# Two fused layers on one core: new constants for the hand-planned order of steps, which place the scatter and gather DMAs of GpSimd otherwise among its other steps

## The chip, the cores and the metric

One Trainium2 chip, of which the kernel uses one core. The metric is the device time of one execution in microseconds; the kernel before was run three times beside this work, and the median of those runs is the time before.

## What is computed

The input is `x`, 16 sequences of 512 tokens with 128 channels. Two layers follow each other, each with a mixer and a mixture of experts on the same normalised input, multiplied together and added to the residual:

```
xn = layernorm(x);  s = rwkv6_mixer(xn);        g = silu(experts0(xn));  x = x + s * g
xn = layernorm(x);  s = attention16heads(xn);   g = silu(experts1(xn));  x = x + s * g
# experts: scores = xn @ router; top 2 of 8; each expert is (silu-gated up, gate) then down, width 256
# experts0: softmax over the two; experts1: sigmoid gate on the input of the expert, and one shared expert
# rwkv6: token-shift mixes (five low-rank "lora" terms), decay = exp(-exp(w)), a 64x64 state per head, group norm, gate
```

## The kernel before

Each sequence is one batch `n` (0 to 15). Per batch and layer the work is cut into steps: tuples `(n, layer, kind, ...)`. A table `DUE` gives each step a due time, worked out by `due_times()` from the constants at the head of the file. One batch is due `PERIOD` = 167.91 after the last, and layer 1 of a batch runs beside layer 0 of the batches behind it. Each engine has a queue of its own, an in-order program: `order(engine)` sorts all steps by `due(step) + LATER[engine][kind]`, and an engine issues for each step what that step has for it, or nothing. So the constants are no waits and no times on the chip: they only set the order of the steps in the five queues (PE, ACT, DVE, POOL, SP). What starts when is up to semaphores.

The kinds that matter here:

- Layer 0's mixer is a chain, `mixin`, `lora`, `decay`, `proj`, `value`, `diag`, `pair`, `level` 0 to 4, `cross128/256/512`, `wkvsum`, `wkv`, `wkvT`, `finish`. A `level` i multiplies 32 small 64x64 products on PE (L740). Between its two halves of 16 stands a fence: PE waits until the last product of the first half has raised a semaphore. Its operand `rk` (two buffers, `mixa` and `rk_odd`) is made in step `decays` i: POOL writes differences (L1140, L1141), ACT takes their exponential (L1028), POOL multiplies it in (L1155, twice).
- Experts. `route` and `rank` find for each token its two places in a list sorted by expert. `scatter` 0 to 7 are eight indirect DMAs that POOL issues (L1112), which write 128 token rows each to those places in HBM (for layer 1 two products `xgate`, L1108, come ahead of the first and the fifth). `fetch` 0 to 3 read the sorted rows back (SP, L558), `weights` read the weights of the block's expert (SP, three DMAs each, L573 to L575), `xT` transposes on PE (L653), `up`, `gate`, `down` are the expert's products, `yout` writes the result to HBM (SP, L584), and `gather` 0 to 7 are eight indirect DMAs of POOL (L1123) that bring each token its two rows. `combine` adds them.
- Layer 1's attention: `smax` (PE L828, row maxima on DVE L1360), `soft` (PE L843, exponential on ACT L1007), `pv` (PE L857), then `headsT` (PE L864), `outT` (PE L613) and `finish` (PE L806), with ACT copies between (L1015, L1017). `mrow` sends the row maxima through two SP DMAs.

The lines that place the steps which the change moves:

```
due[0, "decays", s[2]] = due[s] - DECAYS_BEFORE              # levels; CROSS_BEFORE for cross*
due[layer, "gather", i] = due[layer, "yout", QUADS - 1] + GATHER_AFTER + GATHER_EVERY * i
due[layer, "scatter", i] = due[layer, "rank"] + SCATTER_AFTER + SCATTER_EVERY * i
due[layer, "fetch", m] = max(due[layer, "scatter", 2 * NT - 1] + FETCH_AFTER, due[layer, "xT", m] - FETCH_BEFORE)
due[1, "headsT", g] = soft_at + PV_AFTER + HEADS_AFTER       # outT, finish: LAST_AFTER later each
at -= UNITS0_EARLY                                           # in due(): experts of batch 0, layer 0
return sorted(PLAN, key=lambda s: due(s) + LATER[engine].get(s[2], 0.0))
```

Of the kernel before, what the change touches and what calls it, by code (L numbers as in the profile page):

```python
# [66 lines left out]
PERIOD = 167.91  # L67
MIX_START = 0.91
MIX_EVERY = 5.92
DECAYS_BEFORE = 5.86  # L70
CROSS_BEFORE = 5.77
FINISH_AFTER = 4.27
UNIT_START = 4.02
UNIT_EVERY = 9.78
GATE_AFTER = 2.82
DOWN_AFTER = 8.1
XT_BEFORE = 4.7
WEIGHTS_BEFORE = 17.22
GATHER_AFTER = 8.11
COMBINE_AFTER = 29.52  # L80
YOUT_AFTER = -0.18
NORM0_AT = 100.17
NORMT_AFTER = 4.16
ROUTE_AFTER = 1.7
RANK_AFTER = 4.58
SCATTER_AFTER = 1.7
FETCH_AFTER = 7.18
LAYER1_AFTER = 20.48
NORM1_AFTER = 2.85
ROUTE1_AFTER = 8.52  # L90
# [32 lines left out]
def due_times():  # L123
# [1389 lines left out]
```

## Time and profile before

| | us |
|---|---|
| median of 3 runs | 2964.4 |
| lowest and highest of them | 2952.69, 2973.52 |
| the profiled execution, its own time | 2970.36 |
| span of its core in the profile | 2968.6 |
| PE busy | 2538.9 (86%) |
| DVE, ACT, POOL busy | 1713.8, 1411.3, 996.5 |
| mean granted TensorE clock, share of full | 0.946 |

The profiled execution lies 6.0 us above the median, and 1.8 us of its time lie outside the span. In the views below, times are in us from the start of the span, PE is the matmul engine, PEld its weight load, and square brackets give how long an engine stood idle ahead of an instruction and what the profile names as its releaser.

### The profile page before, as it was taken

The numbers are of one execution on the slowest core, as the hardware profiler recorded it, in microseconds if no ns is written. First come the engines' busy times: TensorE is split into PE (matmuls) and PEld (weight loads), VectorE is DVE, ScalarE is ACT, GpSimd is POOL, SyncE is SP. The second block draws the span as 40 slices with busy tenths as digits, with TensorE's granted clock in tenths as the row PEclk, the third lists the DMA queues.
The fourth block names the chain that finished last, engine by engine and source line by source line (L and its number), as shares of the span: only waits on it lengthen the run. The fifth ranks groups of instructions, "written<-read, shape, count | busy, mean of one in ns | idle before, by whom it ended". The sixth has DMA issues, their size and how long they took to land.

```text
span 2968.6 us, 54716 instructions
## 1 busy us (share of the span) xinstructions
PE 2538.9 (86%) x18122; PEld 1773.5 (60%) x18122; DVE 1713.8 (58%) x4229; ACT 1411.3 (48%) x2613; POOL 996.5 (34%) x1140
## 2 busy tenths in 40 slices
PE   5688898888989888898888989888898888988987
PEld 3456565665656666566665656666566565656644
DVE  3355566565566656656565566656556565565653
ACT  1235454455445454454444445455454454445554
POOL 2433342423433233342323433243342323433201
PEclk6789999999999999999999999999999999999998
DMA  4234333333343333433333333333433333333222
GB/s 132 66 107 116 115 98 109 104 109 110 103 115 98 104 110 104 121 102 99 109 99 110 103 108 92 116 107 108 117 99 102 102 107 109 105 108 89 86 61 67
DMA packets 384820, 306.24 MB, mean 103 GB/s; under 512 B 37440, under 2 KB 376096, under 8 KB 384544
## 3 DMA queue, kind: packets, MB, share of 16 engines
q1 hardware_dynamic: 368160, 269.16, 31.1%
q0 software_dynamic: 16384, 33.59, 4.1%
q8 instruction: 151, 2.47, 0.4%
q14 instruction: 125, 1.02, 0.1%
HBM read 247.15 MB, written 54.39 MB: 102 GB/s over the span
## 4 chain that ended last, share of the span: by engine, by line
PE 64%; issue 12%; ACT 8%; DVE 7%; another core or an unknown queue 5%; POOL 2%; DMA 0%; SPq 0%; ACTq 0%; POOLq 0%; DVEq 0%
PE bank_st L843 7%; PE bank_s L828 7%; PE bank_y L688 6%; PE bank_pv L857 6%; PE bank_h L669 6%; PE bank_mix L740 5%; PE bank_g L669 5%; ACT probs L1007 3%; PE bank_mix L699 2%; DVE rowmax L1360 2%; ACT ks L992 2%; PE bank_mix L709 1%; PE bank_attn L864 1%; PE bank_mix L653 1%
## 5 line engine op out<-in xcount | busy, mean ns | idle before, releaser
L1360 DVE TENSOR_REDUCE rowmax<-bank_s 128x1 f32<-128x512 f32 x1016 | 699.1, 688 | 511.2 <-PE bank_s L828 405.2
L1007 ACT ACTIVATE probs<-bank_st 128x512 f32<-128x512 f32 x992 | 589.7, 594 | 356.6 <-PE bank_st L843 324.0
L843 PE MATMUL bank_st<-qs,ks 128*128 128x512 f32 x992 | 508.7, 513 | 67.2 <-ACT probs L1007 53.5
L828 PE MATMUL bank_s<-ks,qs 128*128 128x512 f32 x1016 | 451.7, 445 | 99.1 <-DVE rowmax L1360 78.4
L828 PEld LDWEIGHTS bank_s<-ks,qs 128*128 128x128 f32 x1016 | 198.9, 196 | 196.0 <-DVE rowmax L1360 141.2
L843 PEld LDWEIGHTS bank_st<-qs,ks 128*128 128x128 f32 x992 | 194.5, 196 | 196.9 <-ACT probs L1007 126.3
L1123 POOL DMA_INDIRECT yg<-ys_d,index x256 | 248.9, 972 | 181.1 <-DMA ys_d<-y_sb 111.5
L688 PEld LDWEIGHTS bank_y<-wbuf,hid 128*128 128x128 f32 x1920 | 260.9, 201 | 61.5 <-DVE hid L1254 27.1
L669 PEld LDWEIGHTS bank_h<-xT_sb,wbuf 128*128 128x128 f32 x1920 | 256.6, 197 | 57.9 <-issue 25.4
L669 PE MATMUL bank_h<-xT_sb,wbuf 128*128 128x128 f32 x1920 | 269.9, 284 | 18.0 <-DVE th L1242 17.2
L688 PE MATMUL bank_y<-wbuf,hid 128*128 128x128 f32 x1920 | 275.3, 288 | 10.7 <-ACT y_sb L932 6.8
L669 PEld LDWEIGHTS bank_g<-xT_sb,wbuf 128*128 128x128 f32 x1920 | 257.7, 196 | 44.6 <-issue 26.7
L924 ACT ACTIVATE th<-bank_h 128x512 f32<-128x512 f32 (+1 forms) x288 | 164.7, 572 | 220.7 <-PE bank_h L669 190.1
L1242 DVE SCALAR_TENSOR_TENSOR th<-th,bank_h 128x512 f32<-128x512 f32 (+1 forms) x288 | 187.8, 652 | 141.4 <-ACT th L924 134.4
L669 PE MATMUL bank_g<-xT_sb,wbuf 128*128 128x128 f32 x1920 | 266.3, 282 | 0.0
L1254 DVE TENSOR_TENSOR hid<-th,bank_g 128x512 f32<-128x512 f32 (+1 forms) x288 | 187.7, 652 | 119.2 <-remote 68.6
L857 PE MATMUL bank_pv<-probs,v 128*32 128x512 f32 x2048 | 252.6, 612 | 1.2 <-ACT probs L1007 1.0
L1070 POOL TENSOR_TENSOR xmixT<-moved,xnT 128x512 f32<-128x512 f32 x80 | 86.8, 1086 | 395.8 <-DVE moved L1284 395.8
L992 ACT ACTIVATE ks<-bank_attn,cols_sb 32x512 fp32r<-32x512 f32 x256 | 173.4, 677 | 36.7 <-PE bank_attn L820 34.2
L1112 POOL DMA_INDIRECT xs_d<-xn,index x128 | 126.2, 986 | 108.5 <-PE bank_mix L758 42.3
L1112 POOL DMA_INDIRECT xs_d<-xgate,index x128 | 127.2, 994 | 35.1 <-issue 26.1
L1155 POOL TENSOR_TENSOR mixa<-kT,expd 128x256 f32<-128x256 f32 x48 | 36.6, 762 | 293.6 <-ACT expd L1028 293.6
(243 smaller groups left out, 3634.5 us busy)
## 6 DMA issues: line engine op xcount, KB each, us to landing
wbuf<-up SPq DMA_DIRECT2D x480, 128.0 KB
wbuf<-gate SPq DMA_DIRECT2D x480, 128.0 KB
wbuf<-down SPq DMA_DIRECT2D x480, 128.0 KB
xs_sb<-xs_d SPq DMA_DIRECT2D x96, 256.0 KB
ys_d<-y_sb SPq DMA_DIRECT2D x96, 256.0 KB
xs_sb<-xs_d SPq DMA_DIRECT2D x32, 192.0 KB
ys_d<-y_sb SPq DMA_DIRECT2D x32, 192.0 KB
x_next<-x SPq DMA_DIRECT2D x16, 256.0 KB, 3.2
```

The costliest lines, as they stand in the source:

```text
L669: last = mm(ps[:, (FT * i + f) * P:(FT * i + f + 1) * P], wbuf[:, load % WRING, part, f * P:(f + 1) * P], rows, start=True, stop=True)
L688: last = mm(bank[YB][:, blk % 4 * P:(blk % 4 + 1) * P], hid[:, NUMBER[n, layer, "up", u] % 4, (FT * i + f) * P:(FT * i + f + 1) * P], wbuf ...
L828: mm(room(s, b)[:], qs[:, slot, q * P:(q + 1) * P], ks[:, slot, j, :], start=True, stop=True).then_inc(filled[b], 1)
L843: mm(room(s, b)[:], ks[:, slot, j, k * P:(k + 1) * P], qs[:, slot, :], start=True, stop=True).then_inc(filled[b], 1)
L857: last = mm(ps[32 * j:32 * j + 32, :], v1_all[:, k, (DK + 1) * (HG * g + j):(DK + 1) * (HG * g + j) + VCOLS], probs[:, slot, j, :], start= ...
L992: last = A(ks[rows, group % RING, j, :], ps[rows, :], ACT.Identity, bias=cols_sb[rows, COL_KONE:COL_KONE + 1])
L1007: A(probs[:, turn % PRING, h % HG, :], ps[:], ACT.Exp).then_inc(emptied[b], 1)
L1112: pool.indirect_dma_start(xs_d[layer][:, :], where, src, None).then_inc(scattered[layer], 16)
L1123: pool.indirect_dma_start(yg[layer][:, k, q, :], None, ys_d[layer][:, :], where).then_inc(gathered[layer], 16)
L1242: v.scalar_tensor_tensor(out=th[:, i % 2, 0:wide], in0=th[:, i % 2, 0:wide], scalar=1.0, in1=bank[HB][:, 0:wide], op0=ALU.add, op1=ALU.mul ...
L1254: v.tensor_tensor(hid[:, i % 4, 0:wide], th[:, i % 2, 0:wide], ps[:, 0:wide], ALU.mult).then_inc(emptied[GB], 1)
L1360: v.reduce_max(rowmax[:, h // HG % 2, NT * (h % HG) + q:NT * (h % HG) + q + 1], content(s, b)[:], AX).then_inc(emptied[b], 1)
```

## The change

Only constants move; no instruction is added or taken away, and no wait.

```
-DECAYS_BEFORE = 5.86            +DECAYS_BEFORE = 4.34
-CROSS_BEFORE = 5.77             +CROSS_BEFORE = 6.35
-FINISH_AFTER = 4.27             +FINISH_AFTER = 7.19
-GATHER_AFTER = 8.11             +GATHER_AFTER = 8.53
-SCATTER_AFTER = 1.7             +SCATTER_AFTER = 1.11
-SCATTER_EVERY = 3.18            +SCATTER_EVERY = 3.16
-FETCH_AFTER = 7.18              +FETCH_AFTER = 6.83
-FETCH_BEFORE = 19.53            +FETCH_BEFORE = 21.15
-HEADS_AFTER = 1.74              +HEADS_AFTER = 2.1
-UNITS0_EARLY = -2.61            +UNITS0_EARLY = -4.82
 LATER['pool']: scatter 0.48 -> 0.21, finish, headsT, xT, value, diag (POOL has nothing in these five)
 LATER['pe']:   wkvT 0.75 -> 1.45
 LATER['act']:  diag, down;  LATER['dve']: attnv, fetch;  LATER['sp']: decay, norm, cross256, cross512
                (these engines have nothing to issue in those steps)
```

`FINISH_AFTER` is not used by `due_times()`.

Put through `due_times()` and `order()`, the new constants give the following in a batch in the middle of the run (s = scatter, g = gather, | = other POOL steps; layer 1's scatters are of batch n, its gathers of batch n-1):

```
POOL, layer 1  before  s0 | s1 s2 | s3 | s4 g0 s5 g1 g2 s6 g3 | g4 s7 g5 g6 g7 |
               after   s0 s1 | s2 | s3 | s4 s5 g0 g1 s6 g2 | g3 s7 g4 g5 g6 g7 |
POOL, layer 0  before  decays2 | g0 | decays3 | g1 g2 g3 g4 | decays4 | g5 g6 g7 |
               after   decays2 | g0 g1 | decays3 | g2 g3 g4 | decays4 | g5 g6 g7 |
POOL, layer 0's scatters: s0 | decays7 | s1 s2 s3 s4 s5 s6 s7, before and after
```

On ACT `decays` 0, 1, 3 and 4 come one to three steps later and `decays` 5 one earlier; on PE four pairs of neighbours change places (`headsT` 3 and `level` 1, `outT` and `level` 2, layer 1's `finish` and a `soft`, `wkvT` and a `smax`); on SP `fetch` goes ahead of the `yout` that it stood behind, in five places; DVE's order stays. In batch 0 ten mixer steps of PE come ahead of an expert step that they stood behind.

## Rows read from the trace of the kernel before

**Rows 1.** The page: busy time by engine, and the chain that ended last by engine.

```profile
PE 2538.9 (86%) x18122; PEld 1773.5 (60%) x18122; DVE 1713.8 (58%) x4229; ACT 1411.3 (48%) x2613; POOL 996.5 (34%) x1140
PE 64%; issue 12%; ACT 8%; DVE 7%; another core or an unknown queue 5%; POOL 2%; DMA 0%; SPq 0%; ACTq 0%; POOLq 0%; DVEq 0%
```

**Rows 2.** Windows: first batch, a middle one; busy by engine, granted clock, DMA.

```profile
31.00:147.00 116.00, 78.58 (x581) 54.75 (x581) 47.46 (x127) 25.87 (x49) 45.08 (x54) 0.72 0.29 86
...
1011.00:1190.00 179.00, 155.58 (x1132) 110.24 (x1132) 106.60 (x263) 88.03 (x164) 62.34 (x72) 0.96 0.37 106
```

**Rows 3.** Groups of PE instructions: busy, mean ns, idle before and its releasers.

```profile
L740 PE MATMUL bank_mix<-mixa 64*64 64x64 f32 x1536 | 65.4, 224 | 8.4 <-PE bank_mix L740 4.6 <-ACT xT_sb L917 0.7 <-POOL mixa L1155 0.3
...
L740 PE MATMUL bank_mix<-rk_odd 64*64 64x64 f32 x1024 | 43.6, 224 | 22.0 <-remote 11.2 <-PE bank_mix L740 6.7 <-issue 3.0
```

**Rows 4.** Waits: who waited for whom, us in total, times, longest.

```profile
PE bank_s L828 <- issue: 16.8, 14, 2.8
...
PE bank_st L843 <- issue: 10.4, 11, 3.2
```

**Rows 5.** Timeline of POOL, `gather` 1 to 4 of layer 0, batch 6.

```profile
1116.33 0.99 POOL L1123 DMA_INDIRECT yg<-ys_d,index  x1
...
1120.12 1.02 POOL L1123 DMA_INDIRECT yg<-ys_d,index  x1 [0.30 <-issue]
```

**Rows 6.** Timeline of PE in the same stretch: `headsT` 3, then `level` 3.

```profile
1109.80 0.63 PE L864 MATMUL bank_attn<-ident_sb,oT 128*128 128x128 f32 x4 [0.37 <-ACT v L957]
...
1119.20 0.68 PE L740 MATMUL bank_mix<-rk_odd 64*64 64x64 f32 x16
1122.14 0.68 PE L740 MATMUL bank_mix<-rk_odd 64*64 64x64 f32 x16 [2.25 <-remote]
```

**Rows 7.** Timeline of all engines around layer 0's scatters (batch 7's).

```profile
1147.49 1.02 POOL L1112 DMA_INDIRECT xs_d<-xn,index  x1 [0.17 <-issue]
...
1155.13 0.96 POOL L1112 DMA_INDIRECT xs_d<-xn,index  x1 [0.30 <-issue]
1157.68 0.60 ACT L1015 ACTIVATE oT<-bank_pv 128x512 f32<-128x512 f32 x1 [5.31 <-remote]
...
1158.33 1.12 PE L864 MATMUL bank_attn<-ident_sb,oT 128*128 128x128 f32 x4 [2.95 <-ACT oT L1015]
```

**Rows 8.** Timeline of all engines around layer 1's first long run of DMAs.

```profile
1044.94 1.00 POOL L1112 DMA_INDIRECT xs_d<-xgate,index  x1 [0.28 <-DMA ys_d<-y_sb]
...
1052.67 0.96 POOL L1123 DMA_INDIRECT yg<-ys_d,index  x1 [0.30 <-issue]
...
1054.69 0.50 PE L843 MATMUL bank_st<-qs,ks 128*128 128x512 f32 x1 [3.25 <-issue]
```

**Rows 9.** Timeline of all engines, `decays` 0 and `level` 0, later `decays` 3.

```profile
1097.06 0.62 ACT L1028 ACTIVATE expd<-moved 128x512 f32<-128x512 f32 x1
...
1097.76 0.84 POOL L1155 TENSOR_TENSOR mixa<-kT,expd 128x256 f32<-128x256 f32 x1 [13.82 <-ACT expd L1028]
...
1098.56 0.84 POOL L1155 TENSOR_TENSOR mixa<-rT,expd 128x256 f32<-128x256 f32 x1
...
1100.03 0.59 ACT L1007 ACTIVATE probs<-bank_st 128x512 f32<-128x512 f32 x1
...
1101.78 1.43 PE L740 MATMUL bank_mix<-mixa 64*64 64x64 f32 x32
...
1116.45 0.60 ACT L1007 ACTIVATE probs<-bank_st 128x512 f32<-128x512 f32 x1 [1.76 <-PE bank_st L843]
```

**Rows 10.** Timeline of all engines around `wkvT` (L613).

```profile
1177.58 0.69 DVE L1360 TENSOR_REDUCE rowmax<-bank_s 128x1 f32<-128x512 f32 x1 [0.59 <-PE bank_s L828]
...
1178.07 0.60 PE L613 MATMUL bank_mix<-ident_sb,kT 128*128 128x128 f32 x4
```

**Rows 11.** Timeline of all engines, `fetch` 2 of layer 0 and its `xT`.

```profile
1057.59 0.44 SPq L558 DMA_DIRECT2D xs_sb<-xs_d  x1
...
1069.06 0.63 PE L653 MATMUL bank_mix<-ident_sb,xs_sb 128*128 128x128 f32 x4 [0.81 <-DVE moved L1284]
```

More of the change, by code:

```diff
@@ L69 @@
 MIX_EVERY = 5.92
-DECAYS_BEFORE = 5.86
-CROSS_BEFORE = 5.77
-FINISH_AFTER = 4.27
+DECAYS_BEFORE = 4.34
+CROSS_BEFORE = 6.35
+FINISH_AFTER = 7.19
 UNIT_START = 4.02
@@ L78 @@
 WEIGHTS_BEFORE = 17.22
-GATHER_AFTER = 8.11
+GATHER_AFTER = 8.53
 COMBINE_AFTER = 29.52
@@ L85 @@
 RANK_AFTER = 4.58
-SCATTER_AFTER = 1.7
-FETCH_AFTER = 7.18
+SCATTER_AFTER = 1.11
+FETCH_AFTER = 6.83
 LAYER1_AFTER = 20.48
@@ L95 @@
 MROW_AFTER = 3.09
-HEADS_AFTER = 1.74
+HEADS_AFTER = 2.1
 LAST_AFTER = 5.4
-SCATTER_EVERY = 3.18
+SCATTER_EVERY = 3.16
 GATHER_EVERY = 1.5
@@ L101 @@
 MIX0_STEP = 0.0
-UNITS0_EARLY = -2.61
+UNITS0_EARLY = -4.82
 SOFT0_EARLY = 0.0
@@ L106 @@
 ROUTE15_EARLY = 4.71
-FETCH_BEFORE = 19.53
-LATER = {'dve': {'up': 1.19, 'gate': 1.0, 'level': 0.61, 'decay': 1.3, 'lora': 0.51, 'rank': 0.96, 'yout': -0.03, 'pv': 1.08, 'headsT': 0.92, 'attnv': 0.21, 'diag': -0.69, 'cross128': -0.85, 'stack': 1.61, 'cross512': -1.5, 'wkvT': 0.22, 'mixed': 0.83, 'wkvsum': 0.17, 'shared': -0.25, 'route': 0.68, 'fetch': 0.12, 'combine': 0.94, 'scatter': -0.91, 'finish': -2.01, 'normT': -0.31, 'weights': -0.97, 'pair': -0.66, 'qk': 0.05, 'xT': 0.18, 'value': -1.11, 'gather': 0.83, 'wkv': 1.02, 'decays': -0.46, 'outT': 0.52, 'down': 0.66, 'proj': -0.01}, 'act': {'soft': -0.4, 'decays': -0.16, 'gate': 0.72, 'finish': -1.63, 'outT': 2.61, 'mrow': 0.8, 'rank': -0.51, 'smax': 0.1, 'shared': -0.63, 'weights': -1.41, 'fetch': 0.93, 'value': 0.47, 'combine': -0.19, 'up': -0.06, 'level': -0.5, 'mixin': 0.06, 'wkvT': 2.81, 'headsT': 0.62, 'cross128': 1.15, 'norm': 2.72, 'mixed': 0.54, 'yout': -0.32, 'gather': 0.75, 'stack': -0.03, 'attnv': 0.27, 'diag': -0.41, 'pv': -1.12, 'lora': 0.98, 'scatter': 0.89, 'down': 0.2, 'normT': 0.17, 'pair': 0.61, 'cross512': 0.01}, 'pool': {'lora': -1.03, 'wkvT': -0.34, 'down0': 1.07, 'headsT': -2.95, 'wkv': 0.87, 'down': -0.67, 'norm': 0.26, 'fetch': -0.44, 'pv': 0.56, 'stack': 1.51, 'gate': -1.54, 'outT': 0.22, 'normT': 0.23, 'soft': 0.86, 'qk': 1.09, 'yout': 0.5, 'cross256': 1.22, 'gather': 0.28, 'level': 5.46, 'value': -0.54, 'up': 1.08, 'smax': 0.59, 'mrow': 0.0, 'cross128': -1.44, 'weights': 0.48, 'combine': 0.14, 'shared': -1.46, 'decay': -0.87, 'diag': 0.67, 'route': 0.92, 'proj': 1.78, 'scatter': 0.48, 'decays': -0.54, 'rank': -1.12, 'xT': -0.02, 'mixed': 1.5, 'attnv': -0.39, 'wkvsum': -1.17, 'pair': -0.8, 'cross512': -0.72, 'finish': -0.57, 'mixin': 1.01}, 'pe': {'down': -0.56, 'soft': -0.2, 'level': 0.0, 'gate': 1.03, 'mixed': -0.07, 'normT': 0.48, 'proj': -0.12, 'wkvT': 0.75, 'up': 0.21, 'attnv': -0.33, 'norm': -0.47, 'diag': -2.09, 'value': -0.57, 'cross256': 1.31, 'pair': -0.57, 'mixin': 1.17, 'wkv': -0.5, 'finish': -0.86, 'mrow': -0.23, 'shared': -1.42, 'fetch': 1.19, 'route': 0.22, 'weights': 2.33, 'yout': 1.2, 'gather': -1.28, 'xT': 0.01, 'rank': 0.39, 'cross128': -0.53, 'wkvsum': 0.78, 'qk': -0.11, 'lora': 0.06, 'scatter': 0.33, 'cross512': 1.26, 'decays': 0.12, 'combine': 0.27, 'decay': 0.06, 'stack': -0.29, 'outT': 0.54}, 'sp': {'soft': 0.1, 'norm': 2.82, 'wkvsum': 2.2, 'finish': 0.27, 'decays': -1.59, 'mrow': -0.49, 'rank': 0.41, 'pair': 2.37, 'stack': 0.26, 'smax': -0.96, 'level': 0.63, 'weights': -1.04, 'gather': 1.03, 'normT': -1.83, 'wkvT': -0.6, 'lora': -0.96, 'pv': -0.41, 'fetch': 2.87, 'up': 0.34, 'attnv': -2.24, 'value': 1.67, 'proj': 3.2, 'yout': 0.01, 'qk': 1.58, 'cross128': 0.14, 'route': 0.54, 'mixin': 2.03, 'xT': 0.98, 'down': -1.0, 'diag': 0.12, 'combine': 0.01, 'decay': 2.0, 'gate': -1.06, 'shared': 0.02, 'mixed': 0.3, 'headsT': -1.99, 'scatter': -0.38, 'cross256': -0.41}}
@@ new lines @@
+FETCH_BEFORE = 21.15
+LATER = {'dve': {'up': 1.19, 'gate': 1.0, 'level': 0.61, 'decay': 1.3, 'lora': 0.51, 'rank': 0.96, 'yout': -0.03, 'pv': 1.08, 'headsT': 0.92, 'attnv': -0.54, 'diag': -0.69, 'cross128': -0.85, 'stack': 1.61, 'cross512': -1.5, 'wkvT': 0.22, 'mixed': 0.83, 'wkvsum': 0.17, 'shared': -0.25, 'route': 0.68, 'fetch': 0.21, 'combine': 0.94, 'scatter': -0.91, 'finish': -2.01, 'normT': -0.31, 'weights': -0.97, 'pair': -0.66, 'qk': 0.05, 'xT': 0.18, 'value': -1.11, 'gather': 0.83, 'wkv': 1.02, 'decays': -0.46, 'outT': 0.52, 'down': 0.66, 'proj': -0.01}, 'act': {'soft': -0.4, 'decays': -0.16, 'gate': 0.72, 'finish': -1.63, 'outT': 2.61, 'mrow': 0.8, 'rank': -0.51, 'smax': 0.1, 'shared': -0.63, 'weights': -1.41, 'fetch': 0.93, 'value': 0.47, 'combine': -0.19, 'up': -0.06, 'level': -0.5, 'mixin': 0.06, 'wkvT': 2.81, 'headsT': 0.62, 'cross128': 1.15, 'norm': 2.72, 'mixed': 0.54, 'yout': -0.32, 'gather': 0.75, 'stack': -0.03, 'attnv': 0.27, 'diag': -0.68, 'pv': -1.12, 'lora': 0.98, 'scatter': 0.89, 'down': -0.92, 'normT': 0.17, 'pair': 0.61, 'cross512': 0.01}, 'pool': {'lora': -1.03, 'wkvT': -0.34, 'down0': 1.07, 'headsT': -3.85, 'wkv': 0.87, 'down': -0.67, 'norm': 0.26, 'fetch': -0.44, 'pv': 0.56, 'stack': 1.51, 'gate': -1.54, 'outT': 0.22, 'normT': 0.23, 'soft': 0.86, 'qk': 1.09, 'yout': 0.5, 'cross256': 1.22, 'gather': 0.28, 'level': 5.46, 'value': 0.04, 'up': 1.08, 'smax': 0.59, 'mrow': 0.0, 'cross128': -1.44, 'weights': 0.48, 'combine': 0.14, 'shared': -1.46, 'decay': -0.87, 'diag': 1.65, 'route': 0.92, 'proj': 1.78, 'scatter': 0.21, 'decays': -0.54, 'rank': -1.12, 'xT': 1.11, 'mixed': 1.5, 'attnv': -0.39, 'wkvsum': -1.17, 'pair': -0.8, 'cross512': -0.72, 'finish': -1.08, 'mixin': 1.01}, 'pe': {'down': -0.56, 'soft': -0.2, 'level': 0.0, 'gate': 1.03, 'mixed': -0.07, 'normT': 0.48, 'proj': -0.12, 'wkvT': 1.45, 'up': 0.21, 'attnv': -0.33, 'norm': -0.47, 'diag': -2.09, 'value': -0.57, 'cross256': 1.31, 'pair': -0.57, 'mixin': 1.17, 'wkv': -0.5, 'finish': -0.86, 'mrow': -0.23, 'shared': -1.42, 'fetch': 1.19, 'route': 0.22, 'weights': 2.33, 'yout': 1.2, 'gather': -1.28, 'xT': 0.01, 'rank': 0.39, 'cross128': -0.53, 'wkvsum': 0.78, 'qk': -0.11, 'lora': 0.06, 'scatter': 0.33, 'cross512': 1.26, 'decays': 0.12, 'combine': 0.27, 'decay': 0.06, 'stack': -0.29, 'outT': 0.54}, 'sp': {'soft': 0.1, 'norm': 4.73, 'wkvsum': 2.2, 'finish': 0.27, 'decays': -1.59, 'mrow': -0.49, 'rank': 0.41, 'pair': 2.37, 'stack': 0.26, 'smax': -0.96, 'level': 0.63, 'weights': -1.04, 'gather': 1.03, 'normT': -1.83, 'wkvT': -0.6, 'lora': -0.96, 'pv': -0.41, 'fetch': 2.87, 'up': 0.34, 'attnv': -2.24, 'value': 1.67, 'proj': 3.2, 'yout': 0.01, 'qk': 1.58, 'cross128': 0.14, 'route': 0.54, 'mixin': 2.03, 'xT': 0.98, 'down': -1.0, 'diag': 0.12, 'combine': 0.01, 'decay': 2.25, 'gate': -1.06, 'shared': 0.02, 'mixed': 0.3, 'headsT': -1.99, 'scatter': -0.38, 'cross256': -2.32, 'cross512': -0.87}}
```

## The prediction

> **What bounds the kernel now.** I read the page first. PE is busy 86% of the span and has 64% of the chain, with 12% "issue" and 5% "another core or an unknown queue" [rows 1]. So PE sets the time, and what can be won is its idle time. The windows say how much that is: in a middle batch PE is busy 155.58 of 179 us, at a granted clock of 0.96, so some 23 us of a batch are idle, while in the first batch, where only one mixer chain is under way, it is busy 78.58 of 116 [rows 2]. Since every queue is in order, a moved step costs or gives something only where PE then stands idle longer or shorter.
>
> The second question was where those 23 us lie. The groups of PE show that the five `level` steps, all of one form and one length, are not treated alike: those that read `rk_odd` (levels 1 and 3) lose 22.0 us over the run, of which the largest part is put down to "remote" and to the step's own fence, those that read `mixa` (0, 2 and 4) only 8.4 [rows 3]. The timeline shows the place: in batch 6 the first half of `level` 3 starts at 1119.20 and the second half at 1122.14, after 2.25 us in which PE waits for its own product behind the fence, released by nobody the profile knows [rows 6]. At that moment POOL is in the fourth of four `gather` DMAs that follow each other, from 1116.33 to 1121.14 [rows 5]. The same shows larger beside the seven `scatter` DMAs of layer 0 in a row, 1147.49 to 1156.09: ACT stands 5.31 us and PE 2.95 us, and all start again together around 1158 [rows 7]; and beside the seven mixed DMAs of layer 1, 1044.94 to 1053.63, where PE stands 3.25 us until 1054.69 [rows 8]. Summed over the run, `smax` and `soft` wait 16.8 and 10.4 us for nothing named, in 14 and 11 waits of up to 2.8 and 3.2 us [rows 4]. I read this as one thing: while POOL issues several indirect DMAs one behind the other, signals between (and within) the engines come late. The trace shows that they fall together, not that one causes the other.
>
> **The change part by part.** Only the order in the queues moves. It does what it is said to do in part: the longest mixed run falls from 7 to 6 and the run of four gathers to three, but the run of 5 grows to 6, and the seven scatters of layer 0 stay as they are. Costs are per batch in the middle, 15 of which count. They are worked out for batch 6, where the rows are.
>
> *Layer 0's gathers (4 to 3 in a row).* What stands to be won is the idle time ahead of the second half of `level` 3: 22.0 us over 16 batches are 1.4 per batch [rows 3]. The nearest row for what a run of three leaves is the `mixa` group, whose `level` 4 stands beside today's run of three: 4.6 us in 16 batches at its fences, 0.3 each [rows 3]. I take -1.1; bounds -1.4 and 0 (the fence may meet a DMA all the same).
>
> *`decays` 0 later on ACT.* Due on ACT at 71.85 it now comes to 73.37, behind `up` 7 (72.42) and the `soft` at 72.62. Today its exponential starts at 1097.06, and the two products on POOL run from 1097.76, 0.08 after its end, to 1099.40; `level` 0 starts on PE at 1101.78 and waits for nothing [rows 9]. That `soft` is the one at 1100.03, ending at 1100.62. From there: 0.62 for the exponential, 0.08, and 1.64 for the products make 1102.96. PE would wait 1.2 us. The cover of 2.4 us that `level` 0 has is used up and more. +1.2; bounds 0 (if `level` 0 is late for another reason anyway) and 1.3.
>
> *`decays` 1, 3 and 4 later.* Only 3 comes near: behind the `soft` at 1116.45, which ends at 1117.05, the same 0.62, 0.08 and 1.64 end at 1119.39, against a start of `level` 3 at 1119.20 [rows 6, 9]. +0.2, bounds 0 and 0.5. On POOL `gather` 1 now stands ahead of `decays` 3, 1.3 us for a DMA and its issue (1116.33 to 1120.12 is three of them [rows 5]); it fills the time in which POOL waits for that exponential, so I cost it at nothing; without that cover it would be 1.3.
>
> *PE's four pairs.* `headsT` 3 waits 0.37 us for ACT today [rows 6]; with `level` 1 ahead of it that wait is filled: -0.4. With `smax` ahead of `wkvT`, the `smax` could start at 1178.07 but its bank is free only when the row maximum ends, at 1178.27 [rows 10]: +0.2. `outT` and `finish` stay within some tenths of their places: 0.
>
> *Layer 1's DMAs.* Runs of 7 and 5 become 6 and 6. If a stall grows with each DMA behind the third, 4 + 2 become 3 + 3: 0. The bounds: the stall of the first run ends 2.0 us after its last DMA's start, 1054.69 against 1052.67 [rows 8], so one DMA less could end it 1.3 earlier, and one more in the second run could lengthen that one by 1.3.
>
> *SP.* `fetch` ahead of `yout`. Each fetch is issued earlier by up to 11 us and nobody waits: `fetch` 2 goes out at 1057.59 and its `xT` starts at 1069.06, held by DVE [rows 11]. `yout`, `weights` and `mrow` behind it in the queue wait for PE or ACT anyway and lose at most its issue, 0.44. 0. If SP had no such waits it would be some tenths.
>
> *Batch 0.* Ten mixer steps come ahead of an expert step. PE has 37 idle us there [rows 2], and the mixer chain is what it waits for, but the steps alternate and most mixer steps would be ready only a little sooner. -3 once; bounds 0 and -10.
>
> The sum: -1.1 + 1.2 + 0.2 - 0.4 + 0.2 + 0 = +0.1 per batch, times 15 is 1.5, less 3: -1.5 us. Against the profiled execution, 2970.4, that is 2968.9; that execution lies 6.0 above the median, so I forecast 2963. What the shorter run of gathers gives, the later exponential takes back.
>
> **A rule of the skill.** The rows show compute engines standing still for 3 to 5 us beside DMAs of POOL [rows 7, 8]. The Trainium skill, "SBUF — State Buffer", section "Who interferes with whom", says the opposite: a DMA never contends with a compute engine, and where POOL's DMAs and DVE meet, it is the DMA that has to wait. By that rule the length of a run costs PE nothing, and there is nothing to win by cutting it. This trace does not bear it out as it stands, though no run yet shows the cause.
>
> **The rivals.**
> *Stalls shrink by more than in proportion.* For it: the first layer 1 run's stall ends with its last DMA [rows 8], so that -1.3 comes there, while today's 5 already stalls PE. Then -1.4 - 1.3 + 1.2 + 0.2 - 0.4 + 0.2 = -1.5 per batch, 15 times -22.5, less 3: 2939. If moreover `level` 0's wait is covered it goes to 2921. Against it: the second run grows.
> *Runs and stalls are not cause and effect.* Then the first term is 0: +1.2 + 0.2 - 0.4 + 0.2 = +1.2, 15 times 18, less 3: 2979. For it: no row shows a mechanism. The skill's rule above would give this.
> *Slower: the second layer 1 run's stall.* The mechanism is that run itself: six DMAs right behind each other, `gather` 3 to 7 around `scatter` 7, with `smax`, whose bank is single, beside it. It decides if each DMA behind the third delays signals by its full 1.3 us and the first run's stall does not shrink, and if in layer 0 the fence of `level` 3 stays caught. +1.3 + 1.2 + 0.2 - 0.4 + 0.2 = +2.5, 15 times 37.5: 3002. For it: the seven scatters cost ACT 5.31 us, far more than four gathers [rows 7]. Against it: today's 7 and 5 cost PE not much more than those 7 alone.
>
> **How the numbers follow.** What a measurement of this kernel can tell from no change is about 1%, 30 us. Forecast 0.50 (own range 2948 to 2978), stalls shrink more 0.22, no cause 0.14, second run 0.14. The rival on the fast side lies about at -1%, so 0.12 of its 0.22 is beyond it, and 0.02 comes from a larger gain in batch 0: faster 0.14. Of the slow one 0.10 is beyond +1%, from 2994 on: slower 0.10. Same 0.76. The range runs from 2932, which leaves out the lower half of the fast rival, to 2990, which leaves out most of the slow one.
>
> **What the profile after would show.** First step: the `rk_odd` group's idle time at L740 falls from 22.0 to some 5 to 8, and no 2.25 us stand between the halves of `level` 3. Second: ahead of `level` 0 PE waits about 1.2 us for POOL, L1155 `mixa`, some 18 us in all where now there are 0.3. Third: the waits of `smax` and `soft` for "issue" stay near 27 us together; above 45 would be the slow rival, below 15 the fast one. `headsT` 0's wait of 2.95 behind the seven scatters stays. The forecast is wrong if POOL is not as free as I take it, so that the gathers reach the fence of another step, or if the clock granted to PE, 0.96 in the middle, moves with how PE is loaded.

## The result, and the profile after

The changed kernel takes 3068.36 us (median of 4 runs, 3063.39 to 3075.46), the kernel before 2958.68 beside it (median of 4, 2952.69 to 2973.52). The ratio is 1.0365 (95% interval 1.0316 to 1.0414): slower by 3.65%, where I had forecast no change. In the experiments below two executions that stood far outside the rest, one of the kernel before at 3108.8 us and one of `u_decays` at 7248.17, are left out of the ratios and means.

The page of after, to be read beside [rows 1]:

```profile
PE 2579.5 (84%) x18122; PEld 1801.1 (59%) x18122; DVE 1729.0 (56%) x4229; ACT 1406.1 (46%) x2613; POOL 997.7 (33%) x1140
...
PE 62%; issue 13%; ACT 9%; DVE 7%; another core or an unknown queue 5%; POOL 4%; DMA 0%; SPq 0%; ACTq 0%; POOLq 0%; DVEq 0%
```

The span is 3061.6, 93.0 us more than before. PE has the same 18122 instructions, but they take 40.6 us more, and the idle time (span less busy) grows from 429.7 to 482.1, 52.4 more. So the loss has two parts of nearly one size, and the first can't be a wait. It goes with the granted clock: windows of after, in the columns of [rows 2] (first batch, a middle one).

```profile
32.00:156.00 124.00, 84.49 (x581) 59.96 (x581) 47.36 (x127) 25.86 (x49) 44.51 (x54) 0.65 0.27 79
...
1057.00:1245.00 188.00, 159.14 (x1133) 112.78 (x1133) 107.68 (x264) 87.66 (x164) 62.80 (x73) 0.95 0.35 101
```

The middle batch has 3.6 us more of PE work for one PE instruction more, at a granted clock of 0.95 in place of 0.96; the first has 5.9 more at 0.65 in place of 0.72. Over the whole span the mean is 0.931 against 0.946.

Where the idle time went is shown by the groups of PE, in the columns of [rows 3] (first two) and for `xT` of layer 0 and layer 1:

```profile
L740 PE MATMUL bank_mix<-mixa 64*64 64x64 f32 x1536 | 69.4, 233 | 66.1 <-remote 28.6 <-PE bank_mix L740 18.7 <-POOL mixa L1155 17.6
L740 PE MATMUL bank_mix<-rk_odd 64*64 64x64 f32 x1024 | 44.5, 227 | 9.0 <-PE bank_mix L740 6.7 <-POOL rk_odd L1155 1.1
L653 PE MATMUL bank_mix<-ident_sb,xs_sb 128*128 128x128 f32 x240 | 40.3, 289 | 25.1 <-DVE moved L1284 14.9 <-issue 5.4 <-ACT xxxT L946 1.7
L653 PE MATMUL bank_attn<-ident_sb,xs_sb 128*128 128x128 f32 x240 | 37.0, 274 | 13.9 <-ACT qs L987 13.8
```

The even levels went from 8.4 to 66.1, the odd ones from 22.0 to 9.0 [rows 3]; both `xT` groups, which before stood at 7.5 and 5.1, grew too. Of the 66.1, 17.6 are the wait of `level` 0 that I had forecast. The other 47 stand at fences ("PE bank_mix" and "remote"), and the timeline of PE and of POOL, batch 6, shows at which:

```profile
1162.44 0.99 POOL L1123 DMA_INDIRECT yg<-ys_d,index  x1
1163.74 0.94 POOL L1123 DMA_INDIRECT yg<-ys_d,index  x1 [0.30 <-issue]
...
1177.28 0.99 POOL L1123 DMA_INDIRECT yg<-ys_d,index  x1
1178.58 0.94 POOL L1123 DMA_INDIRECT yg<-ys_d,index  x1 [0.30 <-issue]
1179.83 0.95 POOL L1123 DMA_INDIRECT yg<-ys_d,index  x1 [0.30 <-issue]
```

```profile
1151.93 0.68 PE L740 MATMUL bank_mix<-mixa 64*64 64x64 f32 x16 [1.05 <-POOL mixa L1155]
...
1163.26 0.68 PE L740 MATMUL bank_mix<-mixa 64*64 64x64 f32 x16
1165.33 0.68 PE L740 MATMUL bank_mix<-mixa 64*64 64x64 f32 x16 [1.39 <-PE bank_mix L740]
1169.91 0.68 PE L740 MATMUL bank_mix<-rk_odd 64*64 64x64 f32 x16
1170.96 0.68 PE L740 MATMUL bank_mix<-rk_odd 64*64 64x64 f32 x16 [0.37 <-PE bank_mix L740]
1178.63 0.68 PE L740 MATMUL bank_mix<-mixa 64*64 64x64 f32 x16
1181.62 0.68 PE L740 MATMUL bank_mix<-mixa 64*64 64x64 f32 x16 [2.31 <-remote]
```

The fence of `level` 3 is free now (0.37 where [rows 6] had 2.25). But `gather` 0 and 1 lie on that of `level` 2 (1.39), and `gather` 5 to 7 on that of `level` 4 (2.31, let go at 1181.62, 0.84 after the last of them ends). The stall was not shortened: it was moved, and caught two fences for one. Summed over the 16 batches from the same timelines, the fences of `level` 2, 3 and 4 idle 1.3, 21.0 and 4.9 us before and 19.3, 6.7 and 28.1 us after. The clock is lost there too: the 4 us behind the stall at 1181.62 are granted 0.57 (window of after, in the columns of [rows 2]).

```profile
1182.00:1186.00 4.00, 4.00 (x30) 2.92 (x28) 3.19 (x7) 1.35 (x3) 1.52 (x2) 0.57 0.01 2
```

### The profile page after: what moved, and what is told of

Read it like the earlier page. It is cut to its first block, busy times and chain, and to the rows that moved or that the text cites. A ratio compares the mean times of both kernels' runs of the same rounds, so it can differ in the third digit from the quotient of the medians.

```text
span 3061.6 us, 54716 instructions
## 1 busy us (share of the span) xinstructions
PE 2579.5 (84%) x18122; PEld 1801.1 (59%) x18122; DVE 1729.0 (56%) x4229; ACT 1406.1 (46%) x2613; POOL 997.7 (33%) x1140
## 4 chain that ended last, share of the span: by engine, by line
PE 62%; issue 13%; ACT 9%; DVE 7%; another core or an unknown queue 5%; POOL 4%; DMA 0%; SPq 0%; ACTq 0%; POOLq 0%; DVEq 0%
PE bank_st L843 7%; PE bank_s L828 7%; PE bank_y L688 6%; PE bank_h L669 6%; PE bank_pv L857 6%; PE bank_mix L740 5%; PE bank_g L669 4%; ACT probs L1007 2%; DVE rowmax L1360 2%; PE bank_mix L699 2%; ACT ks L992 2%; PE bank_g L660 1%; PE bank_mix L709 1%; PE bank_attn L864 1%
## 5 line engine op out<-in xcount | busy, mean ns | idle before, releaser
L843 PE MATMUL bank_st<-qs,ks 128*128 128x512 f32 x992 | 517.8, 522 | 63.9 <-ACT probs L1007 47.8
L688 PEld LDWEIGHTS bank_y<-wbuf,hid 128*128 128x128 f32 x1920 | 267.8, 206 | 63.3 <-DVE hid L1254 27.5
L669 PEld LDWEIGHTS bank_h<-xT_sb,wbuf 128*128 128x128 f32 x1920 | 269.5, 206 | 58.4 <-issue 24.8
L669 PE MATMUL bank_h<-xT_sb,wbuf 128*128 128x128 f32 x1920 | 282.0, 292 | 17.2 <-DVE th L1242 17.2
L688 PE MATMUL bank_y<-wbuf,hid 128*128 128x128 f32 x1920 | 283.2, 293 | 10.1 <-ACT y_sb L932 6.8
L857 PE MATMUL bank_pv<-probs,v 128*32 128x512 f32 x2048 | 271.3, 651 | 1.2 <-ACT probs L1007 1.0
```

The lines of the kernel that those rows point to most:

```text
L669: last = mm(ps[:, (FT * i + f) * P:(FT * i + f + 1) * P], wbuf[:, load % WRING, part, f * P:(f + 1) * P], rows, start=True, stop=True)
L688: last = mm(bank[YB][:, blk % 4 * P:(blk % 4 + 1) * P], hid[:, NUMBER[n, layer, "up", u] % 4, (FT * i + f) * P:(FT * i + f + 1) * P], wbuf ...
L843: mm(room(s, b)[:], ks[:, slot, j, k * P:(k + 1) * P], qs[:, slot, :], start=True, stop=True).then_inc(filled[b], 1)
L857: last = mm(ps[32 * j:32 * j + 32, :], v1_all[:, k, (DK + 1) * (HG * g + j):(DK + 1) * (HG * g + j) + VCOLS], probs[:, slot, j, :], start= ...
```

## The experiments

"Time at full clock" below is the mean over the timed runs of time times granted clock: an estimate of what is left when the clock is taken out, which treats the whole span as if it ran at PE's pace. The last two columns have the kernel under test first, then the kernel before on the same chip. The four groups of four kernels ran on four chips, between which the medians of before differ by up to 1.3% and its times at full clock by 10 us (2795 to 2805), so only ratios are compared between groups.

| kernel | against before (95%) | mean clock | at full clock, us |
|---|---|---|---|
| o_decays | 1.0265 (1.0226 to 1.0303) | 0.943, 0.955 | 2829, 2797 |
| o_dma | 1.0055 (1.0031 to 1.0080) | 0.951, 0.955 | 2799, 2797 |
| o_fetch | 1.0006 (0.9986 to 1.0025) | 0.954, 0.955 | 2795, 2797 |
| o_pe0 | 1.0024 (1.0005 to 1.0043) | 0.951, 0.955 | 2794, 2797 |
| act0 | 1.0138 (1.0102 to 1.0175) | 0.938, 0.947 | 2817, 2805 |
| act134 | 1.0184 (1.0143 to 1.0225) | 0.944, 0.947 | 2845, 2805 |
| pool34 | 0.9980 (0.9959 to 1.0001) | 0.949, 0.947 | 2807, 2805 |
| u_decays | 1.0028 (1.0007 to 1.0048) | 0.943, 0.947 | 2802, 2805 |
| g2222 | 0.9896 (0.9853 to 0.9938) | 0.952, 0.950 | 2782, 2803 |
| act134_g2222 | 1.0038 (1.0015 to 1.0061) | 0.947, 0.950 | 2804, 2803 |
| act0_hot | 1.0088 (1.0049 to 1.0127) | 0.948, 0.950 | 2820, 2803 |
| hot | 0.9896 (0.9844 to 0.9948) | 0.963, 0.950 | 2810, 2803 |
| after_g | 1.0197 (1.0161 to 1.0232) | 0.946, 0.956 | 2817, 2795 |
| after_g_a0 | 1.0118 (1.0067 to 1.0169) | 0.947, 0.956 | 2803, 2795 |
| after_hot | 1.0168 (1.0131 to 1.0206) | 0.959, 0.956 | 2850, 2795 |
| g2222_hot | 0.9829 (0.9795 to 0.9864) | 0.970, 0.956 | 2787, 2795 |

After itself: clock 0.929, time at full clock 2850.

**Which part of the change.** Four kernels, each with one part of it done in the kernel before.

```
o_decays  DECAYS_BEFORE 5.86 -> 4.34
o_dma     GATHER_AFTER, SCATTER_AFTER, SCATTER_EVERY, LATER['pool'] scatter as in the change
o_fetch   FETCH_AFTER, FETCH_BEFORE as in the change
o_pe0     HEADS_AFTER, LATER['pe'] wkvT, UNITS0_EARLY as in the change
```

> The kernel before with DECAYS_BEFORE 4.34 alone. Effective order: on ACT decays 0, 1, 3 and 4 come one to three steps later as in the change; on POOL gather 1 comes ahead of decays 3 and gather 5 ahead of decays 4, so layer 0's gathers go 2, 4, 2. The exponential theory (the later decays on ACT cost the loss: level 0 waits, and the gathers fall on the fences of levels 2 and 4): +60 to +110 us. The contention theory (the earlier fetches on SP are the cause) and the layer 1 theory (the two runs of six): within 15 us of before. The theory that any change of place loses the tuned fit: +20 to +40, as in each of the other three.

> The kernel before with GATHER_AFTER 8.53, SCATTER_AFTER 1.11, SCATTER_EVERY 3.16 and POOL's scatter 0.21 alone. Effective order: layer 1's scatters and gathers as in the change (runs of 6 and 6 in place of 7 and 5); layer 0's gathers 1, 3, 4 (gather 4 behind decays 4); layer 1's mixed copy on ACT one step later. The layer 1 theory: +60 to +110 us. The exponential theory and the contention theory: within 20 us of before. The theory of lost fit: +20 to +40. My old forecast for this part: 0, bounds -20 and +20.

> The kernel before with FETCH_AFTER 6.83 and FETCH_BEFORE 21.15 alone. Effective order: only SP's queue differs, fetch ahead of the yout that it stood behind in five places per batch. The contention theory: +40 or more, with yout and what waits for it later. The exponential theory and the layer 1 theory: within 15 us of before. Lost fit: +20 to +40. My old forecast for this part: 0.

> The kernel before with HEADS_AFTER 2.1, PE's wkvT 1.45 and UNITS0_EARLY -4.82 alone. Effective order: PE's four pairs of neighbours change places per batch, and in batch 0 ten mixer steps come ahead of an expert step. By my old forecast: -0.2 per batch and -3 once, so -6. By the traces of before and after batch 0 alone lost 8 us, from its mixin to that of batch 1, 115.8 to 124.3; if that comes from batch 0's order it shows here: +8 or more, the rest of the loss not. The exponential, layer 1 and contention theories: within 15 us of before.

The four losses are 2.65, 0.55, 0.06 and 0.24%, in sum 3.50 of 3.65%. So three quarters of the loss come with the one constant `DECAYS_BEFORE`, and the contention theory and the layer 1 theory fall. `CROSS_BEFORE` was not moved alone. `o_dma` does not show that the two layer 1 runs of six cost anything: `smax` and `soft` wait 8.8 and 21.1 us there for "issue", 29.9 in sum beside 27.2 before [rows 4], and its time at full clock is 2 us above before's; its layer 0 gathers now come as 1, 3, 4, and the fence of `level` 4 beside that run of four idles 18.4 us, 4.9 before. `o_pe0` loses where I had forecast 6 us won.

The times nearly add, but the waits do not. In `o_decays` PE waits 17.8 us for `mixa` and 28.9 us ahead of layer 1's `xT` (5.1 before, 13.9 in after), while the fence of `level` 2 idles 2.0 us. The 19.3 us of that fence in after appear in none of the kernels with one part. Two parts have to meet there: with `level` 1 ahead of `headsT` 3 on PE, `level` 2 starts 11.33 us after `level` 0 in after, 12.77 in before and 12.77 in `o_decays`; with `gather` 1 ahead of `decays` 3 on POOL there is a second DMA there. In `o_decays`, batch 6, `level` 2 starts just as that pair ends, and nothing stops it (POOL, then PE):

```profile
1130.98 1.00 POOL L1123 DMA_INDIRECT yg<-ys_d,index  x1
1132.28 0.94 POOL L1123 DMA_INDIRECT yg<-ys_d,index  x1 [0.30 <-issue]
```

```profile
1133.25 1.43 PE L740 MATMUL bank_mix<-mixa 64*64 64x64 f32 x32
```

No kernel has those two moves alone together, so this reading is argued from the positions, and that the times add to 3.50 is in part chance.

**What of `DECAYS_BEFORE`.** It moves `decays` on ACT and, against the gathers, on POOL. A term `extra(s)`, added to the key in `order()`, does one alone:

```
act0      engine == "act"  and s[2] == "decays" and s[3] == 0          -> +1.52
act134    engine == "act"  and s[2] == "decays" and s[3] in (1, 3, 4)  -> +1.52
pool34    engine == "pool" and s[2] == "decays" and s[3] in (3, 4)     -> +1.52
u_decays  after, with DECAYS_BEFORE 5.86 and CROSS_BEFORE 5.77
```

> The kernel before with decays 0 alone 1.52 later in ACT's order: its exponential goes behind up 7 and a soft, as in the change; no other queue differs. The step of my forecast: level 0 waits 1.2 us for POOL's mixa in each batch, 15 times 1.2 = +18 us. If each idle microsecond of PE also costs granted clock (DECAYS_BEFORE alone had 2.3 us more idle per batch, 34 us, and 72 us more time): about twice that, +35. If the wait is only part of a stall that moves about: below +8.

> The kernel before with decays 1, 3 and 4 1.52 later in ACT's order (behind one or two soft or stack copies); POOL's order stays. My forecast: +3 us (0.2 per batch). If the gathers of layer 0 are pushed onto the fences of levels 2 and 4 by the later exponentials, since POOL waits for them in order: +15 to +40, and L740 on mixa loses more than 12 us.

> The kernel before with gather 1 ahead of decays 3 and gather 5 ahead of decays 4 on POOL (layer 0's gathers 2, 4, 2 in place of 1, 4, 3); ACT's order stays. My forecast: gather 1 is hidden in the wait for the exponential, 0. If POOL has no such cover, each swap delays decays by a DMA of 1.3 us and level 3 or 4 waits up to that: up to +2.6 per batch, +39. What is left of DECAYS_BEFORE's +72 after the other two kernels of this call should show here.

> The kernel after with DECAYS_BEFORE 5.86 and CROSS_BEFORE 5.77 back. If the parts add up as measured one by one (0.55 + 0.06 + 0.24%): +0.8% against before, +25 us, and L740 on mixa back near 10 us of idle time. If the later exponentials only cost so much because the other parts moved the gathers too: the same. If the other parts lose more together than alone: +1.5% or more.

POOL's part is free (0.9980), as forecast. Both of ACT's parts cost: 1.38 and 1.84%, together more than the 2.65% of `o_decays`, which holds both. `act134` lies above everything that I had named for it (54 us where the highest was 40), and its even levels idle only 8.9 us more, not 12. `u_decays` is 0.28% over before (at most 0.48%), less than the 0.8% that I expected of the three other parts: without the later exponentials, and with `CROSS_BEFORE` back, hardly anything of the loss is left.

`act0` is the clean case. Its group of even levels (the added text makes the line numbers of my kernels 3 to 12 higher: L743 here is L740 of before):

```profile
L743 PE MATMUL bank_mix<-mixa 64*64 64x64 f32 x1536 | 70.5, 236 | 27.9 <-POOL mixa L1158 17.6 <-PE bank_mix L743 8.0
```

The wait is 17.6 us, as worked out, but the loss is 1.38% of 2961.91, 41 us. At full clock it is 12 us; the rest is that the granted clock fell by 0.009.

`act134` loses 54 us, 40 of them at full clock. Its two groups of `level` idle 17.3 and 5.4 us, in sum 7.7 less than before, but this one, 5.1 before, has grown:

```profile
L656 PE MATMUL bank_attn<-ident_sb,xs_sb 128*128 128x128 f32 x240 | 38.8, 284 | 37.2 <-ACT qs L990 37.2
```

It is `xT` 0 of layer 1, whose bank ACT has to empty first. The timeline of all engines in batch 6 shows why ACT is late (`gather` 3 and 4, then the copy):

```profile
1134.07 0.94 POOL L1126 DMA_INDIRECT yg<-ys_d,index  x1 [0.30 <-issue]
...
1134.52 0.40 PE L823 MATMUL bank_attn<-qk_lo,select_sb 128*128 128x512 f32 x1
...
1135.32 0.94 POOL L1126 DMA_INDIRECT yg<-ys_d,index  x1 [0.30 <-issue]
...
1137.15 0.69 DVE L1257 TENSOR_TENSOR hid<-th,bank_g 128x512 f32<-128x512 f32 x1 [3.01 <-remote]
1137.19 0.60 ACT L990 ACTIVATE qs<-bank_attn 128x512 fp32r<-128x512 f32 x1 [4.90 <-remote]
...
1137.94 0.63 PE L656 MATMUL bank_attn<-ident_sb,xs_sb 128*128 128x128 f32 x4 [2.56 <-ACT qs L990]
```

PE's product for that copy is issued at 1134.52 and lasts 0.40; the copy starts at 1137.19, 0.93 after the fourth gather has ended at 1136.26, together with DVE. Before, PE's fence at `level` 3 was let go 1.00 after its fourth gather (1121.14 and 1122.14, [rows 5, 6]). It looks like the same stall. The exponential is later, so POOL's four gathers behind it are, and they fall on another hand-off.

Batch 6 is one of the long cases, though. In before, batches 2 to 15, the wait at `level` 3's fence begins at the same place each time, 3.55 us after the first of the four gathers has started. It ends about 0.5 us before the fourth gather does in seven batches (0.75 to 0.81 us idle), 0.22 us behind it in two (1.49), and 0.94 to 1.00 us behind it in five (2.21 to 2.25). One batch of each of the two shorter kinds:

```profile
941.96 0.68 PE L740 MATMUL bank_mix<-rk_odd 64*64 64x64 f32 x16
943.39 0.68 PE L740 MATMUL bank_mix<-rk_odd 64*64 64x64 f32 x16 [0.75 <-PE bank_mix L740]
...
1297.12 0.68 PE L740 MATMUL bank_mix<-rk_odd 64*64 64x64 f32 x16
1299.29 0.68 PE L740 MATMUL bank_mix<-rk_odd 64*64 64x64 f32 x16 [1.49 <-issue]
```

**Are the gathers in a row the cause, and is the clock?**

```
g2222         POOL: decays 2, g0 g1, decays 3, g2 g3, decays 4, g4 g5, norm, decays 5, g6 g7
act134_g2222  both
hot           ahead of PE's wait in headsT 0:  hot(room(s, misc), 8)
act0_hot      act0, and ahead of rk_done in level 0 (n > 0):  hot(room(s, misc), 4)
+ def hot(ps, count):
+     for _ in range(count):
+         mm(ps[:, 0:P], ones_sb[:].to_broadcast([P, P]), ones_sb[:].to_broadcast([P, P]), start=True, stop=True)
```

> The kernel before with layer 0's gathers on POOL in four pairs: decays 2, g0 g1, decays 3, g2 g3, decays 4, norm, g4 g5 (norm between by due time), decays 5, g6 g7, decays 6. combine has 18 us of slack on DVE's order behind them. If the stall comes from several DMAs in a row: level 3's and level 4's idle time, xT 0 and what else meets it shrink, -1.4 to -2 per batch, and with the clock -20 to -50 us. If single DMAs or pairs delay signals just as much and only the place matters: within 15 us of before, with idle time moved to other steps.

> The kernel before with decays 1, 3 and 4 1.52 later on ACT (which alone cost 1.84%) and the gathers in pairs as in the kernel above. If decays 3 and 4 cost so much because the run of four gathers then reaches ACT's copies for xT 0 (2.6 us, released by ACT qs only 0.9 us after the fourth gather's end): the loss is mostly gone, under +15 us. If the later exponentials cost by themselves: still +40 to +55.

> The kernel before with decays 0 1.52 later on ACT (which alone cost 1.38%, 41 us, for 17.6 us of waits), and with four unused 128-column products written into level 0's own bank ahead of its wait, in batches 1 to 15, so that PE works in that wait. The clock theory (idle time of PE lowers the granted clock, which more than doubles its price): the idle time is filled, the granted clock is back near that of before, +15 to +22 us. If the rest of the loss comes from another source: still about +41. If the products only add work: above +41.

> The kernel before with eight unused 128-column products (about 2.3 us) written into headsT 0's own bank ahead of its wait of 2.95 us per batch for ACT's oT behind the seven scatters. The clock theory: the granted clock rises, and the kernel is faster than before by 5 to 20 us. If PE's clock does not depend on this idle time: 0, or slower by what the products run past the wait.

With the gathers in pairs the kernel before gets 1.04% faster, 20 us of it at full clock, and its odd levels idle 5.9 us where they idled 22.0. The pairs there meet hardly any fence, so this kernel changes the length of the runs and their place at once:

```profile
L745 PE MATMUL bank_mix<-mixa 64*64 64x64 f32 x1536 | 65.4, 224 | 5.2 <-PE bank_mix L745 1.0 <-ACT xT_sb L922 0.7 <-POOL mixa L1160 0.3
L745 PE MATMUL bank_mix<-rk_odd 64*64 64x64 f32 x1024 | 43.6, 224 | 5.9 <-PE bank_mix L745 4.6
```

With the pairs, `decays` 1, 3 and 4 later come to 0.38% over before, 11 us, so the loss of `act134` is mostly gone, as the first theory has it. But measured against `g2222` itself they still cost 1.0038 / 0.9896, 1.4%, and 22 us at full clock where it was 40 without the pairs. The wait for `qs` is gone (37.2 to 4.8 us), while the even levels idle 22.4. So pairs halve the price of the later exponentials at full clock; they don't remove it: the fence of `level` 4 now stands beside a pair and idles 1.23 to 1.30 us in 13 batches, 17.5 us in all.

`hot` shows the clock by itself. It adds work, takes none away, and is 1.04% faster, 31 us where I expected 5 to 20, while its time at full clock is 7 us above before's. (The trace has two PE instructions for each of these products: the eight that are written make 256 in 16 batches. A `level`'s 32 are likewise 16 in the code.) In the kernel before four PE instructions of `cross512` follow `headsT` 0, which had waited 2.95 us [rows 7]. Windows of before, then of `hot`, up to `headsT` 0 and behind it, in the columns of [rows 2]:

```profile
1140.00:1158.00 18.00, 14.94 (x96) 10.09 (x94) 9.25 (x27) 8.42 (x18) 10.71 (x12) 0.99 0.60 175
1158.00:1162.00 4.00, 3.67 (x10) 2.40 (x11) 1.55 (x4) 1.28 (x3) 0.00 (x0) 0.50 0.10 32
```

```profile
1128.00:1146.00 18.00, 16.99 (x113) 12.15 (x111) 9.26 (x28) 8.46 (x19) 10.72 (x12) 1.00 0.60 175
1146.00:1150.00 4.00, 3.60 (x21) 2.91 (x22) 2.81 (x6) 1.98 (x5) 0.00 (x0) 1.00 0.12 36
```

Before, the 4 us behind the wait are granted 0.50, the lower of PE's two levels (1.2 GHz), and hold 10 PE instructions; with the wait filled they are granted 1.00 (2.4 GHz) and hold 21. Summed over the run, the group of `cross512`, of before and then of `hot`:

```profile
L762 PE MATMUL bank_mix<-rk_odd 64*128 64x256 f32 x128 | 48.1, 509 | 4.2 <-POOL rk_odd L1088 3.8 <-DVE scores L1381 0.4
```

```profile
L767 PE MATMUL bank_mix<-rk_odd 64*128 64x256 f32 x128 | 37.9, 419 | 4.2 <-POOL rk_odd L1095 3.8 <-DVE scores L1388 0.4
```

`act0_hot` fills the waits of `level` 0 and leaves 0.88 of `act0`'s 1.38%: 0.5 points back, though the intervals overlap. That is the way the clock theory says, but weaker: +26 us where I expected 15 to 22. The granted clock is 0.948 against 0.950 of before, so what remains stands at full clock (17 us, about the 17.6 us of the wait).

**The same in the changed kernel, and both gains together.** The `extra` of pairs in the kernel after; the same with `decays` 0 alone 1.52 earlier on ACT; after with both fillings; before with pairs and `headsT` 0 filled.

```
after_g      POOL: decays 2, g0 g1, decays 3, g2 g3, decays 4, g4 g5, norm, decays 5, g6 g7
after_g_a0   the same, and engine == "act" and s[2] == "decays" and s[3] == 0 -> -1.52
after_hot    after, hot(..., 4) ahead of level 0 and hot(..., 8) ahead of headsT 0
g2222_hot    before, pairs and hot(..., 8) ahead of headsT 0
```

> The kernel after with layer 0's gathers on POOL in pairs (g0 g1, decays 3, g2 g3, decays 4, g4 g5, norm, decays 5, g6 g7), nothing else. In the kernel after, L740 on mixa is idle 66.1 us, 17.6 of it the wait for decays 0, the rest beside the gathers. If the gathers reaching the fences of levels 2 and 4 make most of the rest: +1.8 to +2.4% against before, in place of +3.65%. If the loss is the later exponentials by themselves: still over +3%.

> The kernel above with decays 0 back at its old place on ACT alone. decays 0 cost 1.38% by itself in the kernel before. If the causes add: 1.2 to 1.5 points less than the kernel above, so +0.4 to +1.0% against before, of which the layer 1 runs and batch 0 are the rest. If level 0's wait is hidden in the kernel after by something else: the same as the kernel above.

> The kernel after with unused 128-column products in PE's waits: four ahead of level 0 (batches 1 to 15), eight ahead of headsT 0. The clock theory: the granted clock rises from 0.929 to about 0.95 and the kernel is 1.5 to 2.5 points faster than after, +1.2 to +2.2% against before. If the clock is not what makes the second half of the loss: +3.2% or more.

> The kernel before with both gains: layer 0's gathers in pairs, and eight unused products in the wait of headsT 0. Each alone gave -1.04%. If they are two causes (signals held up beside runs of DMAs, and granted clock lost to idle time): -1.7 to -2.1%. If both act by way of the same clock dips: -1.0 to -1.4%.

Pairs take 3.65% down to 1.97%, `decays` 0 back to 1.18%. `act134_g2222`, `o_dma` and `o_pe0` make 1.17 together (0.38 + 0.55 + 0.24), but `o_dma` has an order of layer 0's gathers that the pairs undo, so the match shows little. `decays` 0 gave 0.8 points, not 1.2 to 1.5.

Pairs are no cure where they meet a fence. In `after_g` layer 0 has no longer run, and its even levels still idle 55.6 us, 18.1 of them the wait for `decays` 0; the fence of `level` 2 idles 19.3 us (19.3 in after) and that of `level` 4 17.1 (28.1). Batch 6, `level` 2 and `level` 4:

```profile
L745 PE MATMUL bank_mix<-mixa 64*64 64x64 f32 x1536 | 68.4, 231 | 55.6 <-PE bank_mix L745 34.7 <-POOL mixa L1160 18.1 <-remote 1.6
```

```profile
1128.69 0.68 PE L745 MATMUL bank_mix<-mixa 64*64 64x64 f32 x16 [1.30 <-PE bank_mix L745]
...
1142.65 0.68 PE L745 MATMUL bank_mix<-mixa 64*64 64x64 f32 x16 [1.25 <-PE bank_mix L745]
```

So a shorter run makes the stall at a fence shorter, and its place decides whether there is one.

Filling the waits takes 3.65 to 1.68% and leaves the time at full clock where it was, 2850 both times, so those 2 points are clock. PE's busy time says the same: without the fillings (48.4 us) it is 2494.9 us, against 2579.5 for the same instructions in after. The two gains for the kernel before are two causes: 0.9829, nearly the product of 0.9896 and 0.9896 (0.9793). `g2222_hot`, 2872.68 us beside 2925.10, beats both kernels.

## Why the prediction was wrong

- **The sum.** Forecast +0.1 per batch and -3 once, measured 110 us. Two of its steps failed, one effect of a third was not seen, and the clock was not in it.
- **`decays` 1, 3 and 4 later: +0.2.** This is the step that failed, +3 us in the sum where `act134` measured 1.84%, 54 us. I followed each later exponential only to the `level` that reads it. POOL works in order: what stands behind the exponential, the gathers, moves with it. In batch 6 `gather` 5 starts 22.09 us after `level` 0 before and 25.35 after, and `gather` 5 to 7 then lie on the fence of `level` 4 (4.9 us idle before, 28.1 after, over the run). I had costed the order of the queue, not the time of what is queued.
- **"Layer 0's gathers: -1.1", the fence freed.** `level` 3's fence is free (rk_odd 22.0 to 9.0, forecast 5 to 8), so the step did what it says, and it is worth nothing, since the run meets the fences of `level` 2 and 4. My text names this as what would make the forecast wrong, "so that the gathers reach the fence of another step", but gave it no chance or price; the bound of 0 for this step was too kind, for a run that is moved can cost more than it did. The 1.4 us per batch were also taken as if every batch had batch 6's stall; they are five long ones and nine shorter.
- **"`decays` 0 later: +1.2."** Right in its mechanism and size: 17.6 us of waits for POOL `mixa`, 18 forecast. But an idle microsecond of PE is not a microsecond of time here. `act0` shows 41 us for it. The last clause of the prediction names the clock; the sum took it as constant.
- **PE's pairs, `headsT` 3: -0.4.** Right as a wait: the idle time of L864 for ACT `v` falls from 5.7 us (one such wait stands in [rows 6]) to 0.4. `o_pe0`, which has it, is slower all the same, by 7 us. What I did not see is that the same move starts `level` 2 some 1.4 us earlier, onto `gather` 1 in after.
- **Batch 0: -3.** Wrong in sign: its window grows from 116 to 124 us, at 0.65 clock. `o_pe0` holds this order too: from the first `mixin` product (L694) to that of batch 1 it takes 132.5 us, where before takes 129.5 and after 138.0 (`o_decays` 132.3). So about 3 us of the 8.5 come with that part.
- **Layer 1's runs: 0, bounds 1.3 each way.** `o_dma` measured +16 us, within them, and its waits point to layer 0's gathers. SP's `fetch`: 0, measured +0.06%: right.
- **The signs to look for.** The waits of `smax` and `soft` for "issue" are 15.6 and 13.2 us, 28.8 together, as forecast for the middle case. They were the wrong thing to watch: the stall moved to waits that the profile names otherwise. `headsT` 0's wait stayed, as said (L864 for ACT `oT`, 43.9 us before, 42.4 after).
- **The rivals.** The slower one (3002, 0.14) had the right kind of mechanism, a run meeting hand-offs, at the wrong run, and without the clock. Its 3002 leaves out the -3 of batch 0 that the other sums have; by its own terms it is 2999. The Trainium skill's rule ("SBUF — State Buffer", "Who interferes with whom"), that a DMA doesn't contend with a compute engine, would leave `g2222` at before's time; it is 1.04% faster. The section is about SBUF ports. The runs speak against the rule as far as hand-offs between engines go; data paths were not measured.

By size: half of the 93 us between the two profiled executions is time at full clock, 2968.6 x 0.946 = 2808 against 3061.6 x 0.931 = 2850, 42 us; the other half is the clock of 0.931 in place of 0.946. What stays open is why signals are held up beside POOL's indirect DMAs, and why the same place in the same run costs 0.8 us in one batch and 2.2 in another; no run here looks below the fact. `decays` 1, 3 and 4 were not moved one by one, and no run changes the length of the gather runs and leaves their place.

## What to carry to other kernels

Shorter runs on paper are not shorter stalls: when a queue's order changes, follow everything behind the moved step to the time at which it now runs, and look at which hand-off of the bound engine lies there. Shorter runs of GpSimd's indirect DMAs make the stall at a fence shorter; only keeping them off the fence avoids it (55.6 us idle in `after_g` beside pairs, 5.2 in `g2222`). And read the granted clock behind a long wait of PE: if it halves there, the wait costs more than its length, and products that nobody reads, placed in it, can be a gain.

## What the hardware showed

- Beside several indirect DMAs in a row, hand-offs on other engines come late, whether it is PE's own fence or an ACT copy. In the long cases they are let go 0.84, 0.93 and 1.00 us after the last DMA ends; behind the seven scatters ACT starts 1.59 us after it [rows 7]. In other batches of the same kernel the same fence is let go 0.22 us after the last of four gathers or 0.5 us before its end. The fences shown idle 1.25 to 1.39 us beside pairs and up to 2.31 us beside runs of three and four.
- The granted clock halved in the 4 us behind one wait of 2.95 us of PE, in a kernel whose PE is 86% busy, and not when eight small products filled that wait. It was 0.57 in the 4 us behind a wait of 2.31 us in the changed kernel. Filling the first of these in every batch was worth 0.013 of the mean clock and 1.04% of the time; filling that and `level` 0's in the changed kernel, 0.030 and 1.97 points.
